# Layer 1 of a two-layer graph network: GpSimd copies its own row indices, and TensorE sums nodes first in its turn

## The reference

```python
# layer 0: a message for each edge, summed at the node
h = relu(layernorm(x))
m = softplus(softplus(concat(h[row], h[col]) @ W0 + b0) @ W1 + b1) @ W2 + b2
x = x + segment_sum(m, row)

# layer 1: this is what the change is in
h = relu(layernorm(x))
z = h + segment_sum(h[src], dst)            # neighbours, itself among them
z = relu(z @ W1 + b1) @ W2 + b2
z = (z - mean(z)) * rsqrt(var(z) + eps) * gamma + beta   # over all nodes
x = x + h + relu(z)
```

## Time and profile before

| | us |
|---|---|
| median of 3 runs (lowest to highest) | 2215.23 (2206.49 to 2216.25) |
| the profiled execution, its own time | 2211.46 |
| its span, first to last instruction | 2209.4 |
| layer 1, from the first gather's start to the start of its last statistics | 1375.86 to 2119.12 |

### The profile page before, as it was taken

One profiled execution on the slowest core, in us unless ns is written; L12 is line 12 of the kernel. 1 busy time (PEld: TensorE's weight loads), 2 busy tenths in 40 slices (PEclk: granted clock), 3 DMA queues, 4 the chain that ended last, 5 costly groups with the idle time before them and its releaser, 6 DMA issues. The chain is left out here.

```text
span 2209.4 us, 37024 instructions
## 1 busy us (share of the span) xinstructions
PE 1494.2 (68%) x10067; PEld 1073.5 (49%) x10067; DVE 1076.6 (49%) x3310; ACT 967.3 (44%) x2310; POOL 1052.3 (48%) x1004
## 2 busy tenths in 40 slices
PE   0011139999999999999999996255655555555566
PEld 0011127777777777777777775133323233333344
DVE  6899944454444544454444445133333333333344
ACT  0366656666566666666666664011111111111144
POOL 0699954444344343443434331656655565555500
PEclk9999999999999999999999998677777777677775
DMA  1333333434343343434334343222222222222249
GB/s 29 98 117 128 119 91 87 103 80 107 74 107 86 95 102 80 107 87 94 92 89 108 75 107 74 39 48 50 51 42 48 48 45 48 47 45 46 41 143 323
DMA packets 341012, 187.84 MB, mean 85 GB/s; under 512 B 281563, under 2 KB 307560, under 8 KB 340966
## 3 DMA queue, kind: packets, MB, share of 16 engines
q1 hardware_dynamic: 292388, 129.09, 22.5%
q0 software_dynamic: 28224, 32.57, 8.5%
q10 hardware_dynamic: 20354, 25.65, 3.2%
HBM read 131.42 MB, written 55.79 MB: 85 GB/s over the span
## 5 line engine op out<-in xcount | busy, mean ns | idle before, releaser
L784 POOL DMA_INDIRECT fast_gathered<-h_table,fast_gather_i x441 | 420.8, 954 | 625.4 <-PE bank L928 409.0
L1112 POOL DMA_INDIRECT fast_gathered<-h_neighbours_table,fast_index_i x441 | 423.0, 959 | 326.5 <-issue 228.4
L1020 ACT ACTIVATE fast_h<-bank,b_s 128x384 f32<-128x384 f32 (+1 forms) x490 | 300.8, 622 | 330.3 <-PE bank L939 196.5
L1208 ACT ACTIVATE fast_z_in<-node_sums 128x512 f32<-128x512 f32 x49 | 29.3, 597 | 637.4 <-DMA h_table<-prep_normed 621.4
L1193 PE MATMUL bank<-fast_z_in,gw_s 128*128 128x512 f32 x98 | 97.6, 1098 | 298.4 <-ACT fast_z_in L1208 171.9
L1027 ACT ACTIVATE fast_h<-fast_h 128x384 f32<-128x384 f32 (+1 forms) x490 | 273.8, 559 | 0.0
L816 DVE TENSOR_TENSOR fast_message<-bank,b_s 128x192 f32<-128x192 f32 x147 | 52.5, 357 | 437.8 <-PE bank L974 294.9
L1162 DVE BATCH_NORM_STATS2 z_stats<-z_t (+1 forms) x48 | 33.3, 694 | 400.3 <-ACT z_t L1219 290.1
L953 PE MATMUL bank<-fast_h,w_s 128*128 128x384 f32 (+1 forms) x490 | 223.0, 537 | 0.5 <-ACT fast_h L1027 0.5
L928 PE MATMUL bank<-fast_dst_hot,fast_own_rows 128*64 128x128 f32 x1568 | 203.3, 278 | 0.0
L989 PE MATMUL node_sums<-fast_message,fast_hot 128*128 128x80 f32 x1568 | 202.0, 278 | 0.0
(11 more groups left out here) (231 smaller groups left out, 2873.3 us busy)
## 6 DMA issues: line engine op xcount, KB each, us to landing
fast_local<-local_rows SPq DMA_DIRECT2D x49, 576.0 KB
h_neighbours_table<-fast_h_rows SPq DMA_DIRECT2D x49, 320.0 KB
fast_self_rows<-h_neighbours_table SPq DMA_DIRECT2D x49, 320.0 KB
h_table<-prep_normed ACTq DMA_DIRECT2D x49, 256.0 KB, 2.3
fast_own_rows<-h_table SPq DMA_DIRECT2D x49, 256.0 KB
x_plus_h<-fast_x SPq DMA_DIRECT2D x49, 256.0 KB
finish_resid<-x_plus_h SPq DMA_DIRECT2D x49, 256.0 KB
prep_xin<-in_x SPq DMA_DIRECT2D x48, 256.0 KB
```

The lines of the kernel that those rows point to most:

```text
L784: pool.indirect_dma_start(gathered[slot][:, j * D:(j + 1) * D], None, h0_t, bass.IndirectOffsetOnAxis(ap=gather_i[q][:, n:n + 1], axis=0))\
L1020: A(to[at][:, 0:w], psum[:, 0:w], ACT.Exp, bias=b_s[:, :]).then_inc(done, 1)
L1112: pool.indirect_dma_start(gathered[q][:, c * MW:(c + 1) * MW], None, h1_t, bass.IndirectOffsetOnAxis(ap=index_i[q][:, c:c + 1], axis=0))\
```

## The change

In `edges1` the stage `index` is taken from VectorE. GpSimd's `gather` now does the copying in three pieces: it waits until the index slot, the sums and the match of block `b - 4` are done, then three times copies three columns into `index_i[q]`, waits for that copy, and issues three gathers. And on TensorE `sum_nodes` stands first in the list of stages, with the same lags.

```diff
--- before.py
+++ after.py
@@ -1068,6 +1068,8 @@
                         act.preload_act_table_set(EXP_LN_SET)
                         rounds(act, unit_stages(order, LAG), BLOCKS, 2)
 
+        COPIED = 3
+
         def edges1():
 
             cuts = []
@@ -1105,23 +1107,23 @@
                     @block.gpsimd
                     def _(pool):
                         def gather(b, q, turn):
-                            hold(pool, index_ready, b + 1, passed_pool)
+                            wait_from(pool, gather_done[q], 16 * CT * turn, passed_pool)
                             wait_from(pool, nodes_summed, b - RING + 1, passed_pool)
                             wait_from(pool, matched, b - RING + 1, passed_pool)
-                            for c in range(CT):
-                                pool.indirect_dma_start(
-                                    gathered[q][:, c * MW:(c + 1) * MW], None, h1_t,
-                                    bass.IndirectOffsetOnAxis(ap=index_i[q][:, c:c + 1], axis=0))\
-                                    .then_inc(gather_done[q], 16)
+                            for n in range(CT // COPIED):
+                                nc.gpsimd.tensor_copy(index_i[q][:, n * COPIED:(n + 1) * COPIED],
+                                                      far_src[:, bass.ds(b * CT + n * COPIED, COPIED)]).then_inc(index_ready, 1)
+                                hold(pool, index_ready, CT // COPIED * b + n + 1, passed_pool)
+                                for c in range(n * COPIED, (n + 1) * COPIED):
+                                    pool.indirect_dma_start(
+                                        gathered[q][:, c * MW:(c + 1) * MW], None, h1_t,
+                                        bass.IndirectOffsetOnAxis(ap=index_i[q][:, c:c + 1], axis=0))\
+                                        .then_inc(gather_done[q], 16)
                         rounds(pool, [(0, gather)], BLOCKS)
 
                     @block.vector
                     def _(dve):
                         V = nc.vector
-                        def index(b, q, turn):
-                            wait_from(dve, gather_done[q], 16 * CT * turn)
-                            V.tensor_copy(index_i[q][:, :], far_src[:, bass.ds(b * CT, CT)]).then_inc(index_ready, 1)
-
                         def one_hot(b, q, turn):
                             wait_from(dve, nodes_summed, b - 1)
                             for c, (lo, hi) in enumerate(windows):
@@ -1161,7 +1163,7 @@
                             else:
                                 V.bn_stats(z_stats[:, bass.ds(b * 6, 6)], z_t[:, bass.ds(b * TW, TW)])\
                                  .then_inc(stats_done, 1)
-                        rounds(dve, [(0, index), (2, one_hot), (3, pairs), (3, match), (5, stats)], BLOCKS)
+                        rounds(dve, [(2, one_hot), (3, pairs), (3, match), (5, stats)], BLOCKS)
                         dve.wait_ge(stats_done, BLOCKS)
 
                     @block.tensor
@@ -1198,7 +1200,7 @@
                             wait_from(pe, z_ready, b - 1)
                             nc.tensor.matmul(banks[4 + q % 2][:, 0:TW], gw2_s[:, :], hid[q % 2][:, :],
                                              start=True, stop=True).then_inc(post_done, 1)
-                        rounds(pe, [(1, first), (2, second), (0, sum_nodes)], BLOCKS)
+                        rounds(pe, [(0, sum_nodes), (1, first), (2, second)], BLOCKS)
 
                     @block.scalar
                     def _(act):
```

## The result

The changed kernel took 2144.87 us in the median of 4 runs (2142.21 to 2147.49), the kernel before 2211.56 in the same comparison: a ratio of 0.970, 95% interval 0.967 to 0.973. In three later comparisons, on three different chips, the kernel before took 1996 to 1997 us, and in one of these the changed kernel was timed too: 2096.12 us, a ratio of 1.050, interval 1.048 to 1.052. The same change is 3% faster in one comparison and 5% slower in another. A *report* is here the raise of a semaphore by an operation that has ended. It is called late when the engine that waits for it goes on more than 1.5 us after that recorded end, and prompt otherwise.

A forecast was written before the change was run, and what follows sets the result against it. The prediction took a chain of waits as the bound, no engine being busy over two thirds of the span. Gathers at -53 us and the layer's end at -15 gave -68, so 2143, or 2147 in the median; range 2080 to 2225.

The forecast's parts named there:

- The break: GpSimd's stop at each copy between gathers in layer 1: 1.1 us in the loop, 0.57 outside it.
- The rivals of cheap and dear breaks: GpSimd's breaks in the loop: cheap at 0.6 us, 2088 us, chance 0.12; dear at 1.6 us, 2259 us, chance 0.06.
- the 0.8: In the loop, from the copy's end to the next gather: 0.8 us, with one register wait between.
- The end of the layer: Last gather's end to last statistics in layer 1: 16.1 us in place of 31.4, so -15 us.
- TensorE stays the bound: Rival: lateness is TensorE's own slow work, a block saves only 0.65 us, the tail stays; 2185 us, chance 0.17.
- The sum: Whole kernel: -53 us from layer 1's gathers and -15 from its end, -68 us together.
- The TensorE half: Sums first on TensorE: the next round's work, 8.4 us per block, covers reports 3 to 9 us late.
- Reports of sums come late while gathers are being issued.: Layer 1, kernel before: sums reported 3.3 us after recorded end, 31 us in the first block; reason unknown.
- The rival of starved reports: Reports pass only when GpSimd pauses, at `gather`'s wait for `nodes_summed`: 17.25 us a block, +116, 2331 us, chance 0.11.

The follow-up runs named there:

- the copy a series ahead: Changed kernel with one index copy per block, made by GpSimd a series of gathers ahead: 2139.47 us, ratio 0.973; on another chip 2003.76 us, ratio 1.003.
- one copy: Changed kernel with one copy of nine columns per block in place of three: 2141.56 us against 2200.45 for the kernel before, ratio 0.973.
- the new turn: Kernel before with only TensorE's order changed, sums first, VectorE still copying the index: 2180.46 us against 2200.45, ratio 0.990.
- the GpSimd half: Changed kernel with TensorE's old order, the two products ahead of the sums: 2134.93 us against 2200.45 for the kernel before, ratio 0.969.

## Why the prediction was right, and where it was not

The time was forecast at 2147 and measured at 2144.87; the difference to the kernel before at -68 us, and it is -66.7 against the 2211.56 of that comparison. The terms added up in the same comparison. That the forecast held is partly luck: nothing in it said that its main input, a kernel before with late reports, is not a property of the kernel.

*The break.* Forecast 0.15 + 0.15 + 0.8 in the loop and 0.27 behind the copy outside; measured 0.00 + 0.19 + 0.81 and 0.27. A block in the loop was to cost 13.75 and costs 13.66; the gathers 659, and they take 661.0. In that lie three stops of GpSimd for late reports ahead of the loop (gaps of 2.76, 3.74 and 3.37 us in place of 0.47, 8.5 us in all), which the sum didn't have and which cheaper blocks make up for. The rivals of cheap and dear breaks are out. One reading under it was not in its rows: the two operations in the earlier trace rows have 0.16 us between them, not none. The gap between gather and copy, taken at 0.15, is none.

*What the 0.8 is.* I put it down to waits with registers. With the copy a series ahead, in the same loop and with the same kind of wait, it is 0.16 us. But a wait that isn't met costs 0.27 us outside the loop, in the changed kernel too. So it takes both: 0.81 us was seen only where the wait has its count in a register and isn't met on arrival. That step was right in its number and had half of the reason.

*The end of the layer.* Forecast 16.1, measured 14.8, against 31.4 before.

*TensorE stays the bound.* Not in this kernel: TensorE waits 231.3 us for gathers. With one copy or with the copy ahead it comes back: a block stays at 13.5 to 13.6 us whatever GpSimd saves.

*The sum.* -51.3 (gathers) - 16.6 (tail) + 1.6 and + 1.4 (before and behind) = -64.9 us, the difference of the spans.

*The TensorE half.* "A lateness of the report of 3 to 9 us is then covered by the next round's work" failed. Alone the new turn is worth 1%, and the GpSimd half reaches the full gain without it. Where TensorE does run behind, the lateness grows to 18 us. In the changed kernel there is no lateness left to cover from block 12 on, but for block 47.

*"Reports of sums come late while gathers are being issued."* This holds in two comparisons and fails in three others with the same instructions. Late are VectorE's reports too, and the products themselves stand apart. The kernel before takes 157 us more for the gathers of layer 1 with late reports than without (712.3 - 555.1), 17 more in the tail, and 40 more in layer 0, which gathers too (both traces start it within 0.1 us of each other). The changed kernel takes 661.0 and 652.6 us for the gathers: it is nearly the same in both, and the sign of the change comes from the kernel before. TensorE's clock is no rival for that: over the changed kernel's span it was granted 0.899 with late reports and 0.900 with prompt ones.

*The rival of starved reports.* Its mechanism is real on a late chip: the long ones come through when GpSimd stops. Its price is wrong. With one copy, and with the copy ahead, GpSimd does run until its buffers are full and stop, and a block costs 13.5 to 13.6 us, not 17.25. Its sign came true on a prompt chip for another reason: there the breaks are added to a GpSimd that never waited.

*What the experiments point to.* With the copy a series ahead, the kernel is as fast as the change where reports are late (0.973 for 0.970, in different comparisons) and costs 0.3% where they are prompt, in place of 5%. It is the better change, but on a prompt chip it doesn't beat the kernel before.

Open are the cause of the lateness, and what sets a block at 13.5 us under it. That the engines' instructions come too slowly beside the gathers would fit the products that stand apart. Three reports that come within 0.1 us of each other (1787.12, 1787.16 and 1787.20 in the trace of the copy ahead) for work recorded 15 to 17 us earlier speak for reports being held. Neither was tested on a late chip. Nor is it shown whether breaks let reports through: with three of them 6 and 12 sums are late, with one 31, with the copy ahead 28, but the number of breaks and GpSimd's pace changed together.

One thing more is in the traces. They record the updates of semaphores, and where gathers go out, those of the late chips hold far fewer of them for the same instructions: between the first gather and the last of layer 1, 2823 against 8560 for the kernel before, 4340 against 8786 for the changed one, 2142 against 8543 for the copy ahead. Ahead of layer 0 all of these hold 3936 or 3937. So on a late chip records are lost in the same phases in which reports are late. Whether the recording of the trace takes part in the lateness, or both have one cause, was not tested.

## What to carry to other kernels

Before a wait is bought off with work on the engine that issues the transfers, take the profile again, on a second chip: the wait may not belong to the kernel, and the added work stays. A wait of GpSimd for its own operation costs 0.81 us in the loop here where it isn't met on arrival and 0.16 where it is, so issue the operation one unit ahead of its use. And when an engine's operations start apart with "issue" as the only reason, count that as a cost of its own before forecasting what a reordering covers.

## What the runs showed of the hardware that I had not expected

- One kernel, unchanged, took 2211.56 and 2200.45 us in two comparisons and 1996.21, 1997.33 and 1997.14 in three others. A gather takes 0.96 us in both kinds. The granted clock of TensorE in the loop is 0.73 and 0.87 of full speed, at a busy share of 56% and 64%.
- In the first kind, sums were reported up to 32 us after the recorded end of their last product and one-hot matrices 8 us after theirs, while gathers went out. Of 58 sums over 10 us late in six traces, 55 came through 2 to 6 us after a gather's end, with GpSimd stopped. In the three of these traces whose kernel also has a prompt one, about four in ten of the records of semaphore updates are missing against it, nearly all in the two layers.
- 32 more matmul instructions for a block (16 products of one column) cost no time that shows: 1.003 with and without them.
